# GpSimd's three splitting operations in pieces of 512 columns

## The reference

```python
x = x + _L0_xattn_ref(ctx, ctx, _layernorm(x), mask, Wk, bk, Wv, bv, Wq, bq, Wo, bo)
x = x + _L0_ffn_ref(_layernorm(x), ln1_g, ..., w_gate, w1, b1, w2, b2)
x = x + _L1_xattn_ref(_layernorm(x), ctx, Wq, bq, Wk, bk, Wv, bv)
x = x + _L1_ffn_ref(_layernorm(x), w_gate, w_up, w_down)
```

## Time and profile before

| what | us |
|---|---|
| median of three runs | 2086.83 |
| lowest, highest | 2085.33, 2112.68 |
| the profiled execution, its own time | 2095.28 |
| its span in the trace | 2093.5 |
| GpSimd busy in the whole span | 570.9 |
| DVE busy | 1332.8 |
| PE busy | 1770.4 |

### The profile page before, as it was taken

How to read it: one execution, slowest core, us unless ns; L and a number is a source line. 1 busy time by engine, 2 the same in 40 slices (tenths; PEclk the granted TensorE clock), 3 DMA queues, 4 the chain that set the end, 5 groups by cost and what they waited for, 6 DMA issues and landing times. The chain is left out here.

```text
span 2093.5 us, 40227 instructions
## 1 busy us (share of the span) xinstructions
PE 1770.4 (85%) x13889; PEld 1078.1 (51%) x13890; DVE 1332.8 (64%) x2426; ACT 1098.2 (52%) x2041; POOL 570.9 (27%) x479
## 2 busy tenths in 40 slices
PE   7668888999896889997675599999998469989987
PEld 4312222222673444444564488888887245556555
DVE  6478898996565668883575455555454367767753
ACT  6336777878452567775441244444443246546551
POOL 5244899510430223332366000000000422222000
PEclk9869999999997899998675799999999689999999
DMA  6524665410341121113322211111111411111000
GB/s 186 154 87 140 211 197 179 139 65 2 111 125 60 50 81 49 49 35 130 136 102 82 71 51 45 45 46 50 45 45 41 173 41 51 51 52 50 21 11 21
DMA packets 103208, 171.74 MB, mean 82 GB/s; under 512 B 16008, under 2 KB 78368, under 8 KB 98976
## 3 DMA queue, kind: packets, MB, share of 16 engines
q1 hardware_dynamic: 96928, 153.19, 22.9%
q0 software_dynamic: 6144, 16.79, 2.5%
HBM read 103.34 MB, written 61.87 MB: 79 GB/s over the span
## 5 line engine op out<-in xcount | busy, mean ns | idle before, releaser
L1092 DVE TENSOR_REDUCE a_nm<-a_psS 128x2 f32<-128x1024 f32 (+1 forms) x384 | 446.9, 1191 | 51.4 <-PE a_psS L953 38.3
L1072 ACT ACTIVATE a_prob<-a_psE 128x512 f32<-128x512 f32 (+2 forms) x660 | 335.2, 563 | 122.1 <-PE a_psE L975 120.5
L975 PE MATMUL a_psE<-wall 51*128 51x512 f16 (+3 forms) x1024 | 291.7, 359 | 38.1 <-DMA wall<-a_nrow 26.9
L953 PE MATMUL a_psS<-wall 49*128 49x512 f16 (+4 forms) x1024 | 268.2, 369 | 35.3 <-DVE a_nm L1092 22.6
L1710 ACT ACTIVATE ex_hf<-ex_psH,ex_b 128x256 f32<-128x256 f32 x312 | 130.7, 470 | 216.4 <-PE ex_psH L1741 216.4
L1741 PE MATMUL ex_psH<-ex_xT,wall 128*128 128x256 f16 x1872 | 232.1, 274 | 7.5 <-issue 4.1
L1755 PE MATMUL ex_psY<-wall,ex_hl 128*128 x1872 | 229.8, 273 | 1.4 <-DVEq L1661 0.4
L975 PEld LDWEIGHTS a_psE<-wall 51*128 51x128 f16 x1024 | 76.8, 95 | 276.1 <-ACT a_prob L1072 106.5
L1741 PEld LDWEIGHTS ex_psH<-ex_xT,wall 128*128 x1872 | 182.4, 98 | 34.7 <-issue 13.0
L1755 PEld LDWEIGHTS ex_psY<-wall,ex_hl 128*128 128x128 f16 x1872 | 179.3, 98 | 31.9 <-issue 10.9
L1672 DVE CAST ex_hl<-ex_hf 128x512 f16<-128x512 f32 x156 | 66.6, 427 | 182.2 <-ACT ex_hf L1710 180.4
(11 more groups left out here) (282 smaller groups left out, 3160.0 us busy)
## 6 DMA issues: line engine op xcount, KB each, us to landing
s_qk<-wall SPq DMA_DIRECT2D x32, 512.0 KB, 3.2
wall<-s_qk SPq DMA_DIRECT2D x128, 128.0 KB
xall<-in_w SPq DMA_DIRECT2D x16, 1024.0 KB, 11.8
s_ew<-xall SPq DMA_DIRECT2D x16, 1024.0 KB, 9.2
wall<-s_ew SPq DMA_DIRECT2D x16, 1024.0 KB, 10.6
ex_xt<-s_xs SPq DMA_DIRECT2D x39, 256.0 KB, 2.6
s_ys<-ex_yo SPq DMA_DIRECT2D x39, 256.0 KB, 2.2
t_xin<-in_x SPq DMA_DIRECT2D x16, 512.0 KB, 5.2
```

The lines of the kernel that those rows point to most:

```text
L953: last = pe.matmul(psS[:, bank, col:col + n], Q6[s][at:at + SROWS, pr, t * P:(t + 1) * P], K6[s][at:at + SROWS, pr, 0:n], start=True, stop ...
L975: last = pe.matmul(psE[unit % NE][:, col:col + w], K6[s][at:at + EROWS, pr, t * P:(t + 1) * P], Q6[s][at:at + EROWS, pr, S - w:S], start=T ...
L1072: act.activation(prob_of(unit)[:, 0:w], psE[unit % NE][:, 0:w], ACT.Exp, scale=ESC).then_inc(p_ready, 1)
L1092: dve.tensor_reduce(nm[G % NM_BUF][:, t, :, i], psS[:, at:at + 2, 0:n], axis=AX.X, op=ALU.max, negate=True).then_inc(s_free, 1)
```

## The change

For each unit the multiplication, the cast and the subtraction are issued as pieces of 512 columns, one after another, without a wait between the pieces of one operation. The semaphore is raised by the last piece. The waits between the three operations stay. A unit of 2048 columns has four pieces of each, one of 1536 three, one of 512 a single piece as before. The cast from int32 (L864) is not split.

```diff
-                pool.tensor_scalar(raw, raw, scale, None, ALU.mult).then_inc(prep_own, 1)
+                pieces = [slice(at, at + 512) for at in range(0, n, 512)]
+                for piece in pieces:
+                    last = pool.tensor_scalar(raw[:, piece], raw[:, piece], scale, None, ALU.mult)
+                last.then_inc(prep_own, 1)
                 steps += 1
                 pool.wait_ge(prep_own, steps)
                 if i >= 2:
                     pool.wait_ge(pair_out[i % 2], 16 * (i // 2))
-                pool.tensor_copy(pair[:, HIGH], raw).then_inc(prep_own, 1)
+                for piece in pieces:
+                    last = pool.tensor_copy(pair[:, HIGH, piece], raw[:, piece])
+                last.then_inc(prep_own, 1)
                 steps += 1
                 pool.wait_ge(prep_own, steps)
-                pool.tensor_tensor(pair[:, LOW], raw, pair[:, HIGH], ALU.subtract).then_inc(pair_ready, 1)
+                for piece in pieces:
+                    last = pool.tensor_tensor(pair[:, LOW, piece], raw[:, piece], pair[:, HIGH, piece], ALU.subtract)
+                last.then_inc(pair_ready, 1)
```

## The result

Over 20 executions each on the same chips, the change has a median of 2079.24 us (2069.76 to 2086.13) against 2098.39 us (2081.8 to 2131.98) before. The ratio is 0.9916, with a 95% interval of 0.9888 to 0.9944: faster by 0.8%, some 17.6 us by this ratio, inside two per cent. The ratio takes undisturbed executions alone, but among those of before five took 2109.75 to 2112.68 us, while none of the changed kernel is above 2086.13.

A forecast was written before the change was run, and what follows sets the result against it. No engine was at 100%; a loop of GpSimd splitting and loads, 12.2 us a unit, was taken to pace the first attention stage. Terms -3.3 + 6.0 - 5.3 = -2.6 us, from 2086.83 to 2084.2, range 2070 to 2103.

The forecast's parts named there:

- GpSimd's time: Splitting a large unit in the first attention stage: pieces add 1.31 us, so a unit takes 12.81 us on GpSimd.
- DVE gets in between pieces: Large units: L1103 waits at most for one piece, 1.49 us; DVE gains 0.4 to 1.1 us a group.
- no gap between pieces: Rival: pieces pass the port on, so DVE waits for the whole set; sum +9.5 us, 2096.3; chance 0.3.
- The middle: Units 2 to 15 of the first attention stage: GpSimd becomes the pace at 12.81 us a unit, costing +6 us.
- The integer units: Three integer units: L1103 no longer waits for whole GpSimd operations; 5.3 us gained, bounded by 0 and 8.1.
- The first units: First two units of the first attention stage: DVE's waits behind GpSimd mostly go, gaining about 3.3 of 3.5 us.
- Cheap pieces: Rival: pieces add 0.3 us a unit instead of 1.31; sum -15.4 us, 2071.4; chance 0.12.
- The row of maxima gets stuck: Rival: SP's later store and load go right ahead of the maxima PE awaits; six cases +44 us, 2131; chance 0.03.

The follow-up runs named there:

- e5: The changed kernel with all pieces of 256 columns instead of 512; ratio 1.0044 against the kernel before, attention 1 in 425.3 us.
- the halves: The changed kernel with large units in pieces of 1024, integer ones still of 512, run twice; ratios 0.9927 and 0.9913 against the kernel before.
- e9: The kernel before, unaltered, profiled a second time; ratio 1.0014, attention 1 in 420.4 us.
- e3: The changed kernel with only the 16 large units in pieces of 512, the integer units whole; ratio 0.9963 against the kernel before.
- e10: The kernel before with only the multiplication of the three integer units in pieces of 512; ratio 0.9945, attention 1 in 400.0 us.
- e6: The kernel before without the multiplication by the scale in the 19 float units, operations whole; ratio 1.0023, attention 1 in 421.2 us.

## Why the prediction was right or wrong

The sign, the range and "within two per cent" came out; the size did not. A change of -2.6 us was forecast; -15.4 by the profiles and some -17.6 by the ratio were measured. That the median of 2079.24 lies only 5 us from the forecast 2084.2 is luck: the forecast started from a median of three, 2086.83, and the 20 executions of before have 2098.39. By its steps:

**GpSimd's time: right.** 12.81 us a unit was predicted, 12.78 measured; each piece keeps its fixed cost. (The upper bound given for what pieces add, 1.45, was summed wrongly: without any overlap, the rows give 0.59 + 0.53 + 0.56 = 1.67.) e5 confirms the price at twice the pieces (14.55 us; 14.6 expected).

**DVE gets in between pieces: right,** by the timeline at 264.67. The rival "no gap between pieces" falls, and the wait across two fills does not carry over to these pieces. Why not was argued (the reading side is free for a moment) and not tried.

**The middle, +6 us: the failed step.** GpSimd's units did take 4.8 us longer over the 13, as worked out. Groups 5 to 19 took only 1.7 longer than in the first profile, and 7.0 less than in the second. The step that failed is the one from units to groups: I let every group follow GpSimd's unit, by the one wait of the earlier trace rows. L1103 (L1110) of group 5 comes 3.5 us after the start of unit 2 in both kernels. That of group 18, before and in the change:

```profile
356.84 0.54 DVE L1103 TENSOR_SCALAR a_nparts<-a_nm 128x16 f16<-128x16 f32 x1
```

```profile
355.62 0.17 DVE L1110 TENSOR_SCALAR a_nparts<-a_nm 128x16 f16<-128x16 f32 x1
```

Unit 15 started at 351.98 and at 355.71. Before, the group came 4.9 us behind the unit's start, in the change 0.1 ahead of it: the groups slid forward against the units, and so took over little of the 4.8 us. What lets them slide stays open. I also held the landing at 11.8 us, and it fell to 8.6. But no run shows that this helped: the halves have the shortest middle at 11.9 and 10.9, e5 the longest at 8.5 (the pages' rows of loads).

And I priced the stage before by one profile, in which L1103 of the large units always met the multiplication, the cheapest of the three to meet; e9 shows the other case, dearer by 8.7. Against the four profiles with whole large units that went the cheap way (169.7 to 172.0 us, mean 170.7), the three with four pieces (173.7, 172.4, 173.5) are slower by some 2.5 us, not by 6. The whole cast and subtraction are a risk that pieces reduce. How often the kernel before takes the dear way is not measured beyond one profile in five, and e3's 0.4%, some 8 us, is more than these profiles account for: it stays open.

**The integer units, -5.3: mis-sized, it was -10.4** (54.0 to 43.6), beyond the 8.1 I gave as bound. I counted L1103 alone. The rows of before at the first unit, behind the second's L1103 of the earlier trace rows, and at the third:

```profile
401.01 2.58 DVE L1103 TENSOR_SCALAR a_nparts<-a_nm 128x16 f16<-128x16 f32 x1
...
403.77 1.36 DVE L1106 SCALAR_TENSOR_TENSOR a_nparts<-a_nm,a_nparts 128x16 f16<-128x16 f32 x1
...
419.66 0.16 DVE L1106 SCALAR_TENSOR_TENSOR a_nparts<-a_nm,a_nparts 128x16 f16<-128x16 f32 x1
...
430.34 2.13 DVE L1103 TENSOR_SCALAR a_nparts<-a_nm 128x16 f16<-128x16 f32 x1
...
433.53 0.16 DVE L1106 SCALAR_TENSOR_TENSOR a_nparts<-a_nm,a_nparts 128x16 f16<-128x16 f32 x1
```

HIGH to LOW lost 1.5, 2.7 and 1.9 us over the free 1.27, and L1106 another 1.2 at the first unit: 7.3 in all. I put the other 3 us down to the clock: behind each of these waits, with PE busy for only 1.89 of the 3.70 us from 404.0 for one, PE fell for 3.4 us from its level of 2.4 GHz to 1.2 (granted clock 0.50 from 407.7, 421.3 and 435.0; 0.89 in the mean of the window), and it stayed at 2.4 (1.00) in the change, where they are gone. The 7.3 is read off the rows, the 3 is what is left, and no run separates them. I also took the three waits for independent; e10 shows that two of them follow from the first.

**The first units, -3.3: too much.** Up to group 4 the change gained 1.1 us. One part is that GpSimd's unit 1, later by 1.3 + 1.3 us, still ran at group 3, where L1110 waited 1.10 us for a piece of its subtraction and HIGH to LOW took 0.9 more; before, GpSimd was idle by then. The larger part is that the wait of 2.56 us at L1106, though it went, had cost less than its length: from L1103 of group 1 to that of group 2 it was 14.56 us and became 13.74.

**The rest of the 15.4.** 10.5 lie in attention 1. Causal attention (313.4 to 309.4) and the gates (155.4 to 152.9) gave 6.5, and the projections behind attention 1 took 2.0 back (124.3 to 126.3). The second profile of before has 310.4, 153.9 and 123.0 there, so this is mostly between executions.

**"Cheap pieces"** gave -15.4 us, the very difference of the profiles, by a wrong road: pieces are not cheap. **"The row of maxima gets stuck"** is there in small: 22.2 us of waits instead of 13.4, none new over 7.8.

## What to carry to other kernels

When a small DVE operation can be held up behind long GpSimd ones, don't count GpSimd's busy time: look which operation DVE arrives in, since a delay in one group moves its arrival in the next. Cut GpSimd's operations where GpSimd has idle time to pay for the pieces (the integer units: nine pieces, 10 us), and sparingly where it has none; here two pieces of 1024 gave a stage 4.5 us shorter than four of 512, and eight of 256 a slower kernel. Take two profiles of the kernel before when an interaction of two free-running engines is at stake.

## What the runs showed of the hardware that was not expected

A blocked DVE operation costs by the kind of GpSimd operation ahead of it. Behind a multiplication of 2048 columns, the next reduction ran meanwhile (HIGH to LOW at most 2.56 us, has 2.35); behind a subtraction, it did not start until the end (3.99 in e6). Why the two differ no run here shows.

The same transfers land 3.2 us sooner (8.6 against 11.8) where SP issues them apart from the loads of q and k; no byte changed. In the four profiles with large units in pieces of 512 or 256, where SP comes to the load later, the median landing is 8.5 to 9.5 us; in the other ten it is 10.9 to 12.8. No run moved the issue alone. And halving GpSimd's work on the large units (e6) lengthened their stage by 9.1 us against the first profile, and by 0.8 against the second.
